# A graph convolution and a mixture of experts on one core: from tile 16 on, the first expert matrix comes by GpSimd's indexed transfer

## The reference, cut to what matters

```python
x = x + gnn(layernorm(x), edges)                  # first half
z = layernorm(x)                                  # [6250, 256]
logits = z @ gate_w + gate_b                      # 16 experts
vals, idx = top_k(logits, 2); share = softmax(vals)
h = relu(z @ w1[e] + b1[e])                       # w1[e]: 256 x 512
expert_out = h @ w2[e] + b2[e]                    # w2[e]: 512 x 256
moe = sum(share * expert_out[idx])
x = x + layernorm(z + moe) * gamma + beta
```

## Time and profile before

| | |
|---|---|
| runs, us | 880.44, 886.51, 890.98 (median 886.51) |
| the profiled execution's own time, us | 891.48 |
| its span, first to last instruction, us | 889.7 |
| TensorE busy | 744.3 us (84%) |
| VectorE, ScalarE, GpSimd busy | 75%, 53%, 32% |
| expert stage, first to last `up` | 397.8 to 815.8 us |
| mean DMA traffic | 217 GB/s |
| w1 issues (L328 holds w2's as well) | 89 from ACT, 512 KB each |

### The profile page before, as it was taken

How to read it: one execution, slowest core, us unless ns; L and a number is a source line. 1 busy time by engine, 2 the same in 40 slices (tenths; PEclk the granted TensorE clock), 3 DMA queues, 4 the chain that set the end, 5 groups by cost and what they waited for, 6 DMA issues and landing times.

```text
span 889.7 us, 21308 instructions
## 1 busy us (share of the span) xinstructions
PE 744.3 (84%) x6322; PEld 641.1 (72%) x6322; DVE 671.5 (75%) x1830; ACT 475.8 (53%) x1199; POOL 280.9 (32%) x313
## 2 busy tenths in 40 slices
PE   4555788888885776898899999999999999998893
PEld 3555355555555766777787899999998899997682
DVE  6999799999953687877765677777776677775497
ACT  5995677877726666744433344444444344443253
POOL 9400000000000457777744345445432222223010
PEclk9999699999987576569999999999999999999797
DMA  9840444545535934359988899999899999993999
GB/s 268 232 149 1 129 152 145 171 154 166 158 100 208 230 122 141 126 176 305 303 240 251 236 275 265 261 263 267 265 270 329 278 261 262 266 265 115 353 312 199
DMA packets 156241, 192.82 MB, mean 217 GB/s; under 512 B 78235, under 2 KB 125262, under 8 KB 153036
## 3 DMA queue, kind: packets, MB, share of 16 engines
q1 hardware_dynamic: 128056, 113.07, 45.3%
q10 hardware_dynamic: 14440, 47.37, 16.1%
q0 software_dynamic: 13632, 31.03, 11.0%
HBM read 151.05 MB, written 40.34 MB: 215 GB/s over the span
## 4 chain that ended last, share of the span: by engine, by line
PE 47%; DVE 25%; SPq 11%; issue 10%; DMA 4%; ACT 2%; DVEq 0%; ACTq 0%; POOL 0%; POOLq 0%
PE PS L1300 16%; PE PS L1312 15%; DVE W L1361 10%; SPq L723 7%; DVE W L1427 5%; PE PS L1338 4%; DVE W L1392 3%; DMA R<-xs 3%; PE PS L1190 2%; PE PS L1205 2%; PE PS L1218 2%; SPq L726 2%; SPq L320 1%; PE PS L1094 1%; PE PS L1058 1%
## 5 line engine op out<-in xcount | busy, mean ns | idle before, releaser
L1300 PEld LDWEIGHTS PS<-R,W 128*128 128x128 f32 x1808 | 218.9, 192 | 27.2 <-DVE R L1646 20.4
L1300 PE MATMUL PS<-R,W 128*128 128x128 f32 x1808 | 223.0, 276 | 16.2 <-DVE R L1646 14.4
L996 ACT ACTIVATE R<-PS,b1T 128x128 f32<-128x128 f32 x350 | 102.9, 367 | 226.6 <-PE PS L1300 224.6
L1312 PE MATMUL PS<-W,R 128*128 x904 | 216.0, 383 | 0.0
L612 POOL DMA_INDIRECT ys<-W,R x113 | 109.9, 973 | 234.6 <-DVE W L1698 229.2
L1312 PEld LDWEIGHTS PS<-W,R 128*128 128x128 f32 x904 | 165.1, 193 | 18.1
L1361 DVE TENSOR_TENSOR W<-R,W 128x3136 bf16<-128x3136 bf16 (+1 forms) x104 | 156.8, 1562 | 1.1 <-PE PS L1074 1.1
L894 ACT ACTIVATE W<-PS 128x1024 f16<-128x1024 f32 x104 | 106.3, 1023 | 37.9 <-PE PS L1094 33.3
L605 POOL DMA_INDIRECT xs<-W,slot_i x98 | 100.5, 1025 | 79.3 <-DVE slot_i L1526 51.0
L1094 PE MATMUL PS<-W,table 114*128 114x512 f16 x208 | 66.6, 404 | 25.9 <-DVE W L1392 25.5
L597 POOL MEMSET R<- 128x261 f32 x1 | 0.3, 317 | 227.1 <-PEq L1136 227.1
(11 more groups left out here) (267 smaller groups left out, 1034.7 us busy)
## 6 DMA issues: line engine op xcount, KB each, us to landing
W<-in_L_ffn_w ACTq DMA_DIRECT2D x89, 512.0 KB
W<-in_L_ffn_w SPq DMA_DIRECT2D x40, 512.0 KB, 8.7
W<-key_rows SPq DMA_DIRECT2D x26, 784.0 KB
R<-xs SPq DMA_DIRECT2D x113, 130.5 KB
W<-ys SPq DMA_DIRECT2D x4, 2048.0 KB, 12.6
R<-xs SPq DMA_DIRECT2D x224, 32.0 KB
XH<-in_x SPq DMA_DIRECT2D x6, 896.0 KB, 11.7
W<-xs SPq DMA_DIRECT2D x116, 32.0 KB
```

The costliest lines, as they stand in the source:

```text
L996: last = act.activation(HT3[:, u, j, :], up_out(u, j), ACT.Relu, bias=b1T[:, ds(e, 1), j])
L1300: last = nc.tensor.matmul(up_out(u, j), W1S[b][:, k, j * P:(j + 1) * P], XT3[:, u, k, :], start=(k == 0), stop=(k == 1))
L1312: last = nc.tensor.matmul(PS[:, 6 * u, 0:C], HT3[:, u, j, :], wt2(e * W2COLS, j), start=(j == 0), stop=(j == 3))
```

## The change

From tile 16 (`W1_POOL`) on GpSimd brings w1, by an indirect transfer with one index per partition: partition p gets row 128 e + p of w1 seen as 2048 rows of 4 KB. DVE works the indices out (`w1_rows`): where tile t has the expert of tile t-4, whose matrix is in the same buffer, it adds 1.0e6 to the row's number, which is past the bound, and such rows are skipped. SP issues w1 only for tiles 0 to 15, and ACT no longer issues any. GpSimd's fetch of tile t+4 stands ahead of `add_beta` and of the `send`, which is now that of tile t-1 in iteration t. `send` has a bound as well: rows whose place is `TRASH` or later are skipped. SP's wait for the table moves from its w1 loads to its row loads. Some semaphores of DVE are merged, which is left out below; the order of DVE's instructions there stays.

```diff
--- before.py
+++ after.py
@@ -68,6 +68,8 @@
 XBUFS, OBUFS, HBUFS = 4, 11, 14
 TABLES_T = 12
 SOON, SOON_G, SOLO = 20, 3, 11
+W1_POOL = 16
+NO_LOAD = 1.0e6
 XNBUFS = 3
 X_AT = E * WCOLS * 4 - 2 * GT * C * 4
 TRASH = 2 * NT * P
...
@@ -285,6 +287,9 @@
         topi = sb("topi", [P, GT, 8], u32)
         SLOT = sb("SLOT", [P, NT, 2], fp32)
         oh = sb("oh", [P, 2, GT, E], fp32)
+        oh_flat = oh[:, :, :, :].rearrange("p k j e -> p (k j e)")
+        w1_row = oh_flat[:, 0:MT].bitcast(i32)
+        same_e = oh_flat[:, MT:2 * MT - W1_POOL]
         cnt_in = sb("cnt_in", [P, GT + 1, E], bf16)
         posq = sb("posq", [P, GT, E], fp32)
         prodq = sb("prodq", [P, GT, E], fp32)
...
@@ -451,6 +454,7 @@
         tab_ready = sem("tab_ready")
         tab_turned = sem("tab_turned")
         tables_out = sem("tables_out")
+        w1_rows_set = sem("w1_rows_set")
         soon_out = sem("soon_out")
 
         def x_loads(g):
...
@@ -466,6 +470,7 @@
         x3_in = [sem(f"x3_in{b}") for b in range(XBUFS)]
         ROWS_IN = 16 * 5
         w1_in = [sem(f"w1_in{b}") for b in range(W1BUFS)]
+        w1_fetched = [sem(f"w1_fetched{b}") for b in range(W1BUFS)]
         rows_in = sem("rows_in")
         b2_in = sem("b2_in")
         x_turned = sem("x_turned")
...
@@ -611,7 +615,7 @@
                     pool.wait_ge(o_ready, t + 1)
                     nc.gpsimd.indirect_dma_start(
                         out=ys[:, :], out_offset=bass.IndirectOffsetOnAxis(ap=home[:, h:h + 1], axis=0),
-                        in_=O3[o], in_offset=None).then_inc(o_sent[o], 16)
+                        in_=O3[o], in_offset=None, bounds_check=TRASH - 1, oob_is_err=False).then_inc(o_sent[o], 16)
 
                 for g in range(NDG - 1):
                     pool.wait_ge(slots_ready, g + 1)
...
@@ -628,11 +632,27 @@
                     nc.gpsimd.tensor_tensor(XH[:, t, :], XH[:, t, :], beta_bc, ALU.add).then_inc(beta_added, 1)
                     pool.wait_ge(beta_added, t + 1)
 
+                def fetch_w1(t):
+                    b = t % W1BUFS
+                    pool.wait_ge(mm1_done, t - W1BUFS + 1)
+                    nc.gpsimd.indirect_dma_start(
+                        out=W1S[b].rearrange("p k f -> p (k f)"), out_offset=None,
+                        in_=w1.rearrange("e (p k) f -> (e p) (k f)", k=2),
+                        in_offset=bass.IndirectOffsetOnAxis(ap=w1_row[:, t:t + 1], axis=0),
+                        bounds_check=E * P - 1, oob_is_err=False).then_inc(w1_fetched[b], 16)
+
                 for t in range(MT):
+                    if t + W1BUFS >= W1_POOL and t + W1BUFS < MT:
+                        if t + W1BUFS == W1_POOL:
+                            pool.wait_ge(w1_rows_set, 1)
+                        if t + W1BUFS == SOON:
+                            pool.wait_ge(w1_rows_set, 2)
+                        fetch_w1(t + W1BUFS)
                     if 16 <= t < 16 + NT:
                         add_beta(t - 16)
-                    if t >= DG[NDG - 1][1]:
-                        send(t)
+                    if t > DG[NDG - 1][1]:
+                        send(t - 1)
+                send(MT - 1)
 
                 pool.wait_ge(base_stored, 16 * len(FADD))
                 for g in FADD:
...
@@ -731,10 +751,8 @@
                     load(t)
                     load_w1(sp, t, expert_of(mybir.EngineType.SP, t))
                 for t in range(MT):
-                    if t < SOON:
+                    if t + W1BUFS < W1_POOL:
                         sp.wait_ge(mm1_done, t + 1)
-                        if t + W1BUFS == SOON:
-                            sp.wait_ge(tables_out, 4)
                         load_w1(sp, t + W1BUFS,
                                 expert_of(mybir.EngineType.SP, t + W1BUFS))
                     if t + XBUFS < MT:
...
@@ -742,6 +760,7 @@
                         sp.wait_ge(kept_ready, t + 1)
                         sp.wait_ge(home_ready, t + 1)
                         if t + XBUFS == SOON:
+                            sp.wait_ge(tables_out, 4)
                             for b in range(XNBUFS):
                                 sp.wait_ge(xn_sent[b], sends(max(g for g in range(NDG) if g % XNBUFS == b)))
                             sp.wait_ge(pads_in, 16 * (E + 1))
...
@@ -1006,19 +1025,10 @@
 
                 act.activation(warm[:, 0:1], ones1[:, :], ACT.Exp)
                 ratio_of(0)
-                expert = {}
                 for t in range(MT):
                     if t == SOON:
                         act.wait_ge(tables_out, 4)
-                    if t < SOON + W1BUFS:
-                        expert[t] = expert_of(mybir.EngineType.Activation, t)
-                    if t >= SOON and t + W1BUFS < MT:
-                        n = t + W1BUFS
-                        expert[n] = expert_of(mybir.EngineType.Activation, n)
-                    relu(t, expert[t])
-                    if t >= SOON and t + W1BUFS < MT:
-                        load_w1(act, t + W1BUFS, expert[t + W1BUFS])
-                    del expert[t]
+                    relu(t, expert_of(mybir.EngineType.Activation, t))
                     if t + 1 < MT:
                         ratio_of(t + 1)
                     keep(t)
...
@@ -1288,7 +1298,10 @@
                 def up(t):
                     u, b = t % 2, t % W1BUFS
                     pe.wait_ge(x_turned, t + 1)
-                    pe.wait_ge(w1_in[b], 16 * (t // W1BUFS + 1))
+                    if t < W1_POOL:
+                        pe.wait_ge(w1_in[b], 16 * (t // W1BUFS + 1))
+                    else:
+                        pe.wait_ge(w1_fetched[b], 16 * ((t - W1_POOL) // W1BUFS + 1))
                     if t == 1:
                         pe.wait_ge(prefix_read, NDG - 1)
                     if t >= 2:
...
@@ -1638,6 +1650,12 @@
                     nc.vector.tensor_scalar(again[:, SOON:MT], PS[:, 7, 3 * P:3 * P + m], iota_p[:, :], -1.0e6, ALU.is_gt, ALU.mult
                                             ).then_inc(tables_out, 1)
 
+                def w1_rows(a, b):
+                    s, r = same_e[:, a - W1_POOL:b - W1_POOL], w1_row[:, a:b]
+                    link(nc.vector.tensor_tensor(s, et_bc[:, a:b], et_bc[:, a - W1BUFS:b - W1BUFS], ALU.is_equal))
+                    link(nc.vector.tensor_scalar(s, s, NO_LOAD, iota_p[:, :], ALU.mult, ALU.add))
+                    nc.vector.scalar_tensor_tensor(r, et_bc[:, a:b], float(P), s, ALU.mult, ALU.add).then_inc(w1_rows_set, 1)
+
                 def turn_x(t):
                     u, b = t % 2, t % XBUFS
                     dve.wait_ge(x3_in[b], ROWS_IN * (t // XBUFS + 1))
...
@@ -1720,6 +1738,8 @@
                         route(NDG - 1)
                     elif t == 2:
                         place(NDG - 1)
+                    elif t == 3:
+                        w1_rows(W1_POOL, SOON)
                     elif t == 4:
                         tables_a()
                     elif t == 5:
...
@@ -1736,6 +1756,8 @@
                         tables_d()
                     elif t == TABLES_T + 1:
                         tables_e()
+                        dve.wait_ge(tables_out, 4)
+                        w1_rows(SOON, MT)
                 weigh_out(MT - 1)
 
                 def stats(g):
```

More of the change, by code:

```diff
@@ L432, in build @@
         x_added = sem("x_added")
-        dve2 = sem("dve2")
         var2 = sem("var2")
@@ L442, in build @@
         logits_read = sem("logits_read")
-        masked2 = sem("masked2")
         counted = sem("counted")
@@ L476, in build @@
         ratio_ready = sem("ratio_ready")
-        denom_ready = sem("denom_ready")
-        share_ready = sem("share_ready")
+        share_step = sem("share_step")
         first_ready = sem("first_ready")
@@ L1449, in _ @@
                 nc.vector.tensor_scalar(coef[:, :, 2:4], coef[:, :, 2:4], 0.5, None, ALU.mult).then_inc(coef_ready, 1)
-                link = linker(dve, dve2)
+                link = linker(dve, dve_step, sum(link.state))
                 def widest(q):
@@ L1508, in route @@
                         for k in range(2):
-                            nc.vector.tensor_scalar(oh[:, k, n - 1, :], oh[:, k, n - 1, :], rowmask[:, :], None,
-                                                    ALU.mult).then_inc(masked2, 1)
-                        dve.wait_ge(masked2, 2)
+                            link(nc.vector.tensor_scalar(oh[:, k, n - 1, :], oh[:, k, n - 1, :], rowmask[:, :], None,
+                                                         ALU.mult))
                     nc.vector.tensor_tensor(cnt_in[:, GT - n:GT, :], oh[:, 0, 0:n], oh[:, 1, 0:n], ALU.add).then_inc(counted, 1)
@@ L1673, in share_of @@
                     dve.wait_ge(ratio_ready, t + 1)
[L1674 to L1677, removed]
+                    nc.vector.tensor_scalar(denom[:, b:b + 1], ratio[:, b:b + 1], 1.0, None, ALU.add).then_inc(share_step, 1)
+                    dve.wait_ge(share_step, 2 * t + 1)
```

(2 more changed lines are left out.)

## The result

The changed kernel takes 901.28 us (median of six runs, 891.27 to 909.25) against 887.68 for the kernel before (six runs): a ratio of 1.0127, 95% interval 1.0093 to 1.0162, or 11.3 us slower (8.3 to 14.4). The ratio is taken without the run of 909.25, a slow one; the two medians lie 13.6 us apart. The forecast was 880.0, the upper end of the range 901.

A forecast was written before the change was run, and what follows sets the result against it. TensorE is full in the expert stage's steady part, so gains lie in its gaps; -5.7 - 1.6 - 0.5 + 0.3 + 1.0 = -6.5 from 891.48 gives 885.0, 4.97 lower 880.0 us as a median; range 872 to 901.

The forecast's parts named there:

- E: GpSimd's turn of fetch, `add_beta` and `send`, 3.77 or 3.30 us against TensorE's 3.513: +1.0 us, ends 0 and 9.2.
- the high bound: GpSimd's turn at 3.77 us against TensorE's 3.513: loses 0.26 a tile, up to 12.6 us by iteration 64.
- The free time: Slack between a fetch's landing and the `up` that needs it: 3.4 to 6.8 us, hiding GpSimd's lag.
- Two of the signs: Wrong if a fetch takes over 1.2 us, or `up` waits for w1 at tiles 43 to 68, with data first.
- R1: Rival, slower: GpSimd becomes the bound, its period 4.01 us through contention with DVE, ending at 898; chance 0.24.
- A: SP loses the w1 loads of tiles 16 to 23, so rows are issued earlier: -5.7 us, ends -6.65 and -1.0.
- the smaller burst: Three w1 loads in 4 us at the change of issuer, moved to tile 16, instead of five: charged 1.0 us.
- B: Bytes not moved, 50 of 97 fetches without data, one beside the third store: -1.6 us, ends 0 and -4.79.
- R3: Rival, all of it comes, with 50 fetches fewer: -6.65, -4.79, -0.5 and 0.3 us, ending at 875; chance 0.26.
- C: Tail: the last `send`, 2.41 us from issue to landing, writes nothing: -0.5 us, ends 0 and -2.41.
- D: DVE's added `w1_rows` instructions, mostly in its idle time: +0.3 us, 2.8 without idle time.

The follow-up runs named there:

- a_send_free: The changed kernel without the bound on `send`: 880.88 us, 0.996 of the kernel before.
- a_no_wait: The changed kernel, both bounds kept, without GpSimd's wait for its own `add_beta`: 880.33 us, 0.995 of the kernel before.
- b_spare: The kernel before with one more indirect GpSimd transfer a tile in iterations 12 to 55, all rows skipped, nobody waiting for it: 887.45 us, 1.0016.
- second pair of profiles: Both kernels run again without edit: the changed kernel 898.65 us, 1.0153; the kernel before 886.16 us, 0.9997.
- b_act16: The kernel before with ScalarE taking over w1 from SP at tile 16 instead of tile 24: 883.33 us, 0.9985.
- a_no_wait_all: The changed kernel without GpSimd's wait for its own `add_beta`, and with every fetch carrying data: 879.92 us, 0.9956 of the kernel before.

## Why the prediction was wrong

**E failed.** It asked the right question, GpSimd's turn against TensorE's 3.513, but put the turn at 3.30 to 3.77 where it was 4.00 on average, and then gave +1.0 us to what cost 17.8 (0.6 and 17.2 from tile 24 to 72). Three terms were off:

- The gap behind the addition was left between 0.30 and 0.77, as if either could be. It was 0.79. I did not ask what the 0.77 of the earlier trace rows was made of: in that trace a wait for VectorE stands in an instruction of its own (L611) ahead of `send`, and 48 of the 49 `send` behind an addition start 0.71 us after it. Nor did I ask what the bound on `send`, which I had costed at nothing, would put ahead of it. `a_send_free` and `a_no_wait` show that this alone decides: at 0.40 or 0.17 the turn fits. The instruction L611 in the kernel before, once for each addition (lengths in ns):

```profile
L611 POOLq EVENT_SEMAPHORE  x49: 17/17/17, 474.7 to 648.6; - x49
```

- Fetch, addition and `send` took 1.07, 0.78 and 1.03 on average instead of 0.96, 0.73 and 0.98. That is 0.2 more, on top of the 0.26 by which the high bound was too long already.
- The free time was larger than 3.4 to 6.8: a lag of 8.4 us behind the end of `up` cost nothing, one of 9.1 (tile 36) did. But this gave nothing back: at each change from skipped to real fetches (tiles 43, 55, 68) 1.8 to 2.4 us were lost, and in the skipped stretches between them the lag grew again. Of the 17.2 us, 12.0 were lost at tiles with data and 5.2 at skipped ones.

Two of the signs pointed elsewhere: the forecast was to be wrong above all if a fetch takes more than 1.2 us, but 93 of the 97 took less; and the first tiles to wait (36 to 42) have fetches without data.

**R1 had the end right and the cause half right.** It gave 898 with a chance of 0.24, and its period of 4.01 is the measured 4.00. VectorE's instructions with two inputs do meet GpSimd's: `base_of` rose from 0.475 to a mean of 0.578 us (VectorE's groups from 490 to 650 us), by the trace to 0.756 where it lies over an addition and not at all elsewhere:

```profile
L1705 DVE SCALAR_TENSOR_TENSOR gW_all<-W,R,gW_all 128x256 f32<-128x256 f32 x42 | 24.3, 578 | 0.1
```

That agrees with the section "Who interferes with whom" of the Trainium skill's page "SBUF — State Buffer". But the additions and `base_of` overlap in `b_spare` and `a_no_wait` too (0.95 and 0.96 for the addition), with no loss. Dearer transfers and the port make 0.2 us of the period, the wait about 0.5; without the wait the period fits in spite of the port.

**A's stall went in every profile; what that is worth is open.** Tiles 17 to 24 lost 0.0 for 6.65 (at most 0.5 in any version with GpSimd's fetch), and tiles 13 to 17 lost 2.5 more: the smaller burst that I charged with 1.0. Net -4.1 for the -5.7 of the sum. But in the second pair of profiles tiles 13 to 24 lost 4.7 against 4.9, so the size is not settled. In medians, the versions with GpSimd's fetch on time gain 0.4 to 0.6%; the earlier change of issuer by itself (`b_act16`) gains nothing that can be told, so no run shows that this gain is A's. Where the Trainium skill's "DMA: Bandwidth & Descriptors" (section "Issuing engines are not separate DMA queues") calls issue time usually small beside the transfer, the profile shows SP 4.07 us a tile.

**B** was -2.2 for -1.6 in this pair of profiles, which is within the spread of the stores' losses (1.0 to 5.8 with w1 from SP and ACT), and `a_no_wait_all` shows no gain from the bytes: R3's reason falls with it. **C** was -0.5 and came out at +0.2: the last `send` starts 0.71 us behind its wait, not 0.27. **D** shows no cost: tiles 13 to 17 lost 0.6 in `a_no_wait`, which has the same `w1_rows`.

**What to do with the change.** `a_no_wait`, the changed kernel less one wait, beats both: 880.33 us, 0.5% below the kernel before.

## What to carry to other kernels

Where a queue is given one more task per tile, add up its whole turn, gaps included, and compare it with the pace of the engine that bounds the tile: half a microsecond of gap in a turn of 4.0 made 1.3% slower out of 0.5% faster here. A small edit that costs nothing on an idle queue (the bound, 0.9999 by itself) can decide on a full one. And where the spans of two profiles agree while the runs do not, compare them from a point in the program, not from the start.

## What the runs showed of the hardware

- An indirect transfer of GpSimd starts some 0.7 us after the last instruction of its sequencer that waited ahead of it: 0.71 in 48 of the 49 `send` behind an addition in the kernel before, 0.72 to 0.74 in all 49 of the changed kernel, behind the move that waits for the addition, 0.71 in the tail. Where that wait was over early, this time ran beside the addition, and 0.17 (`a_no_wait`) or 0.28 us (`b_spare`) were left between the two. A transfer that held the wait itself started 0.27 us behind it.
- A fetch whose 128 rows are all skipped takes GpSimd as long as one that moves 512 KB: the line of the fetch in the changed kernel (shortest, median and longest in ns) has 97 of nearly one length; the median is 1.041 us for the 47 with data and for the 50 without. Skipping saves traffic and landing time, not issue time: by the last of its 16 semaphore updates a skipped fetch landed 1.1 to 3.4 us after its end (median 1.6), one with data 3.5 to 7.1 (median 4.6).

```profile
L638 POOL DMA_INDIRECT W<-in_L_ffn_w,oh x97: 1036/1041/1310, 447.4 to 802.7; - x97
```

- TensorE is as full at 165 GB/s as at the 264 of the earlier trace rows; a window of `a_no_wait`, columns as above:

```profile
480.00:640.00 160.00, 160.00 (x1095) 150.70 (x1094) 120.86 (x410) 66.45 (x228) 132.27 (x135) 1.00 0.63 165
```

- Who starts first decides what VectorE costs a scatter. In the kernel before, 13 scatters overlap one of VectorE's additions with two inputs in SBUF that take 0.95 or 1.22 us: the 7 that started during the addition took 1.41 to 1.71 us, the 6 that started ahead of it 0.96.
